# Attention and channel-mix layer: single k levels in DRAM, heads 4 to 7 held back, batch 1's features and casts moved into period 0

## The chip, the cores and the metric

One NeuronCore of a Trainium2 chip runs the whole kernel. The metric is device time in microseconds of one execution; lower is better. The engines are TensorE (PE), VectorE (DVE), ScalarE (ACT), GpSimd (POOL) and SyncE (SP, which here only issues DMAs). TensorE's clock has two levels, 2.4 GHz (granted clock 1.00) and 1.2 GHz (0.50).

## The reference, cut to what matters

The input x has 8 batches of 512 tokens by 128 channels. Attention has 16 heads of 8 channels. A score is a sum of three terms, and the softmax over it is causal:

```
q, k, v = x @ qkv_w.T                                  # (b, 16 heads, 512, 8)
scores  = alpha * tanh(q.k / beta)
scores += sigmoid(lam) * tanh(x@hex_w.T).tanh(x@hex_w.T) / 2          # "hamming", same for all heads
scores += sum_de hexc_i[d] * M_h[d,e] * hexc_j[e] / 6 * ...           # "lattice", hexc = tanh(x@q6_w.T)
x = layernorm(x + softmax(causal(scores)) @ v @ out_w.T)
r = sigmoid(mix_r(x) @ W_r.T); kk = relu(mix_k(x) @ W_k.T)**2
x = layernorm(x + r * (kk @ W_v.T))
```

## The kernel before, in words

**Levels.** To use bf16 matmuls at fp32 precision, q, k and the features are split into three bf16 levels each: hi, the cast of the whole; rest (whole minus hi); mid, the cast of the rest; lo (rest minus mid). The code has functions `hi`, `rest`, `mid`, `lo` with (batch, kind), kind being Q, K, J (features of the key side) or G (features of the query side, with the lattice map applied). VectorE does hi and mid, GpSimd rest and lo. A score matmul contracts 72 rows: 3 levels of q times 3 levels of k times 8 channels. Biases (hamming, lattice and a shift) contract 111 rows.

**The way through DRAM.** The levels lie in `parts`. SP writes them to DRAM (`to_dram`: q_rows, k_rows, j_rows, lattice_i, hamming_i) and loads them back into `q_stack`, `k_stack`, `i_stack`, `j_stack` in the order of the 72 or 111 rows (`load_stack`). Row (level l, channel d, copy c) of q_stack holds level l of q. Before, the same row of k_stack holds level (l + c) mod 3 of k, and for that k_rows has five levels (0, 1, 2, 0, 1), written in two DMAs. Heads are loaded in three groups: 0 to 3, 4 to 7, 8 to 15. A batch's stacks are double buffered.

**Steps.** A batch is 18 steps (pairs of heads), called a period. In step t TensorE runs the biases of pair t-1 on top of its scores in PSUM, the scores of pair t+1 ("ahead"), one unit of side work (`units_at`: transposes of x, projections q2, k2, features F, G, values v, and the post-attention work of the batch before) and the probability-by-value products that are due. In steps of AHEAD_FIRST the scores come ahead of the side work. Each PSUM pair has three buffers, so the scores of pair t wait until VectorE has finished pair t-3. ScalarE does tanh of pair t, then exp of pair t-3; VectorE adds scores and biases (`main`, L1210); GpSimd masks. Side units share one PSUM bank, `side_bank`: each waits until the one before has been read. The `FIRST` tables of VectorE and GpSimd say which level operation runs in which step of period 0.

**The start.** The prologue makes batch 0's levels and stacks (`first_stacks` on SP; ACT issues part of the G loads), and projects batch 1's q and k. `busy` issues matmuls whose result nobody reads. `scores(0, 0, 0)` waits for `first_qk`, the first biases for `first_g`, and `scores(0, 0, 4)` for `second_in` (heads 4 to 7 of q, k and G). The features of batch 1 are the unit F2 of the prologue, its G unit comes in step 1 of period 0. Engines run their instructions in the order written.

## Time and profile before

| | us |
|---|---|
| median of 3 runs | 377.19 |
| lowest, highest | 373.98, 377.36 |
| the profiled execution | 374.27 |
| its span, first to last instruction | 372.5 |
| mean granted clock | 0.981 |

The profiled execution is 1.77 us longer than its span and lies 2.9 us under the median of the runs; its times are in microseconds from the span's start. Period 0 is taken from its first tanh (31.03) to the first tanh of batch 1 (72.99). The timeline gives start, duration, engine, line and operation; what stands in brackets is the idle time before it and what ended it ("issue": nothing that the profile shows, which can be a DMA). A row of windows has the busy time and count of PE, PEld (weight loads), DVE, ACT and POOL, then granted clock, mean busy share of the 16 DMA engines, and GB/s.

### The profile page before, as it was taken

How to read it: one execution, taken by the hardware profiler on the slowest of the kernel's cores; microseconds unless marked ns; L12 is line 12 of the kernel's file. 1: busy time of each engine (PE TensorE's matmuls, PEld its weight loads, DVE VectorE, ACT ScalarE, POOL GpSimd, SP SyncE). 2: the span in 40 equal slices, each digit the busy share in tenths (PEclk: the TensorE clock that was granted, in tenths of full speed). 3: DMA queues.
4: the chain of work that ended last, by engine and by line, in shares of the span. 5: the costliest groups of instructions: out<-in, count | busy, mean ns of one | idle time of the engine just before them, and what ended most of it. 6: DMA issues, size and time to landing. Idle time of an engine off the chain costs nothing.

```text
span 372.5 us, 10894 instructions
## 1 busy us (share of the span) xinstructions
PE 344.4 (92%) x4181; PEld 224.4 (60%) x4181; DVE 317.2 (85%) x535; ACT 302.5 (81%) x338; POOL 241.3 (65%) x438
## 2 busy tenths in 40 slices
PE   8877896999999999999999999999999999999883
PEld 8563453566565656656576656665665666556573
DVE  4856989899999998999989999999889868976854
ACT  2322798798889978999899888997999999999712
POOL 8412848763888668865888388866885546554452
PEclk9988999899999999999999999999999999999997
DMA  4365586876763674456735775357546740210010
GB/s 114 58 219 166 178 250 192 270 220 183 198 202 102 187 203 139 128 177 194 202 117 146 182 206 163 103 161 187 157 127 185 196 136 3 59 31 2 2 30 28
DMA packets 41305, 54.01 MB, mean 145 GB/s; under 512 B 4230, under 2 KB 35974, under 8 KB 39670
## 3 DMA queue, kind: packets, MB, share of 16 engines
q1 hardware_dynamic: 36326, 50.76, 47.5%
q10 hardware_dynamic: 4928, 2.56, 2.8%
q8 instruction: 33, 0.54, 0.6%
q14 instruction: 18, 0.15, 0.1%
HBM read 38.69 MB, written 14.61 MB: 143 GB/s over the span
## 4 chain that ended last, share of the span: by engine, by line
PE 49%; DVE 15%; ACT 14%; issue 12%; POOL 8%; POOLq 0%; DVEq 0%; ACTq 0%
PE raw L556 20%; PE sums L556 12%; PE side_bank L556 12%; ACT probs L921 8%; ACT probs L916 6%; DVE probs L1210 5%; PE side_bank L684 4%; POOL probs L1090 2%; POOL x L1132 2%; POOL x L1128 2%; DVE parts L1244 2%; DVE bn L1298 1%; POOL rstd L1120 1%; DVE res L1310 1%; DVE parts L1249 1%
## 5 line engine op out<-in xcount | busy, mean ns | idle before, releaser
L1210 DVE SCALAR_TENSOR_TENSOR probs<-probs,scal,raw 128x1024 f32<-128x1024 f32 x144 | 182.1, 1274 | 19.5 <-PE raw L556 18.6
L916 ACT ACTIVATE probs<-raw 128x1024 f32<-128x1024 f32 x144 | 147.5, 1024 | 29.9 <-PE raw L556 23.8
L921 ACT ACTIVATE probs<-probs 128x1024 f32<-128x1024 f32 x144 | 151.8, 1057 | 0.0
L1090 POOL TENSOR_SCALAR_AFFINE_SELECT probs<-probs 128x128 f32<-128x128 f32 x256 | 72.6, 307 | 68.2 <-ACT probs L921 66.6
L556 PE MATMUL raw<-q_stack,k_stack 72*64 72x64 bf16 (+4 forms) x1024 | 89.2, 236 | 6.3 <-DVE probs L1210 4.7
L556 PE MATMUL raw<-i_stack,j_stack 111*128 111x64 bf16 (+4 forms) x640 | 88.4, 276 | 2.9 <-issue 1.3
L556 PEld LDWEIGHTS raw<-q_stack,k_stack 72*64 72x64 bf16 (+1 forms) x1024 | 50.1, 105 | 47.3 <-issue 21.1
L556 PE MATMUL sums<-probs,values 128*32 128x224 f32 (+3 forms) x1280 | 70.8, 343 | 1.2 <-POOL probs L1090 1.2
L556 PEld LDWEIGHTS raw<-i_stack,j_stack 111*128 111x128 bf16 (+1 forms) x640 | 46.2, 100 | 34.7 <-issue 14.1
L556 PEld LDWEIGHTS sums<-probs,values 128*32 128x32 f32 x1280 | 32.0, 109 | 29.5 <-issue 10.9
L1110 POOL TENSOR_TENSOR parts<-whole,parts 128x512 bf16<-128x512 f32 x30 | 34.8, 1167 | 6.8 <-DVE parts L1249 6.0
L1097 POOL TENSOR_TENSOR whole<-whole,parts 128x512 f32<-128x512 f32 x22 | 26.5, 1203 | 16.9 <-DVE parts L1244 16.9
L1078 POOL TENSOR_SCALAR_AFFINE_SELECT probs<-probs 128x1024 f32<-128x1024 f32 x15 | 17.2, 1149 | 5.6 <-ACT probs L921 5.6
L556 PE MATMUL sums<-ident 128*128 128x128 f32 x114 | 17.5, 313 | 1.6 <-POOL ident L1033 1.6
L1084 POOL TENSOR_SCALAR_AFFINE_SELECT probs<-probs 64x1024 f32<-64x1024 f32 x15 | 17.1, 1139 | 2.8 <-POOL probs L1078 2.8
L556 PEld LDWEIGHTS sums<-ident 128*128 128x128 f32 x114 | 16.7, 227 | 3.0 <-POOL ident L1033 1.6
L1097 POOL TENSOR_TENSOR whole<-feats,parts 128x512 f32<-128x512 f32 x8 | 9.5, 1187 | 11.9 <-DVE parts L1244 11.9
L1276 DVE COPY sums_sb<-sums 128x512 f32<-128x512 f32 x15 | 10.4, 690 | 7.9 <-PE sums L556 7.7
L1244 DVE CAST parts<-whole 128x512 bf16<-128x512 f32 x22 | 15.9, 722 | 0.2
L1120 POOL TENSOR_TENSOR rstd<-var_eps,minus_half 128x4 f32<-128x4 f32 x14 | 14.7, 1047 | 1.2
L1249 DVE CAST parts<-whole 128x512 bf16<-128x512 f32 x30 | 15.2, 524 | 0.0
L556 PE MATMUL side_bank<-w_r_mix,x1T 128*128 128x128 f32 x112 | 13.6, 275 | 0.0
(167 smaller groups left out, 399.7 us busy)
## 6 DMA issues: line engine op xcount, KB each, us to landing
q_stack<-q_rows SPq DMA_DIRECT2D x16, 288.0 KB
k_stack<-k_rows SPq DMA_DIRECT2D x16, 288.0 KB
q_stack<-q_rows SPq DMA_DIRECT2D x24, 192.0 KB
k_stack<-k_rows SPq DMA_DIRECT2D x24, 192.0 KB
i_stack<-lattice_i SPq DMA_DIRECT2D x24, 144.0 KB
i_stack<-hamming_i SPq DMA_DIRECT2D x24, 144.0 KB
i_stack<-hamming_i SPq DMA_DIRECT2D x47, 72.0 KB
i_stack<-lattice_i SPq DMA_DIRECT2D x15, 216.0 KB
```

Of the source, the lines that this page charges most:

```text
L556: return nc.tensor.matmul(o, lhsT, rhs, start=start, stop=stop, **kw)
L916: nc.scalar.activation(pair_probs(t), raw[:, t % PSUM_PAIRS, :].rearrange("p (u i) -> p u i", u=2), ACT.Tanh).then_inc(tanh_done, 1)
L921: nc.scalar.activation(pair_probs(t), pair_probs(t), ACT.Exp).then_inc(exp_done, 1)
L1078: nc.gpsimd.affine_select(out=v, in_=v, compare_op=ALU.is_ge, fill=0.0, base=SQUARE, pattern=[[0, 2 * T // SQUARE], [1, SQUARE]], channel_ ...
L1084: nc.gpsimd.affine_select(out=low, in_=low, compare_op=ALU.is_ge, fill=0.0, base=0, pattern=[[0, 2 * T // SQUARE], [1, SQUARE]], channel_m ...
L1090: last = nc.gpsimd.affine_select(out=block, in_=block, compare_op=ALU.is_ge, fill=0.0, base=SQUARE, pattern=[[0, 2], [1, SQUARE]], channel ...
L1097: nc.gpsimd.tensor_tensor(whole[:, kind, :], feats[:] if kind == J else whole[:, kind, :], parts[:, kind, 0, :], ALU.subtract).then_inc(re ...
L1110: nc.gpsimd.tensor_tensor(parts[:, kind, 2, :], whole[:, kind, :], parts[:, kind, 1, :], ALU.subtract).then_inc(lo_done[kind], 1)
L1120: nc.gpsimd.tensor_tensor(rstd[:], var_eps[:], minus_half[:], ALU.pow).then_inc(rstd_done, 1)
L1210: v.scalar_tensor_tensor(out=o, in0=o, scalar=scal[:, 2:3], in1=raw[:, t % PSUM_PAIRS, :].rearrange("p (u i) -> p u i", u=2), op0=ALU.mult ...
L1244: v.tensor_copy(parts[:, kind, 0, :], feats[:] if kind == J else whole[:, kind, :]).then_inc(hi_done[kind], 1)
L1249: v.tensor_copy(parts[:, kind, 1, :], whole[:, kind, :]).then_inc(mid_done[kind], 1)
```

## The change

- k_rows keeps three levels and is written in one DMA. A load of k_stack is now three DMAs of 24 rows each in all head groups (one of 72 rows before for heads 0 to 3 and 4 to 7): row (l, d, c) holds level l by its block, so the pairing of q and k levels is complete again, in another order.
- SP waits for all of `first_g` ahead of the loads of heads 4 to 7. The Q and K loads of heads 8 to 15 follow at once, then the write of batch 1's Q levels, then G of heads 8 to 15.
- F2 leaves the prologue; step 1 of period 0 does the features of batch 1 as F1, and G1, xT2, q2, k2 come one step later each. The two `busy(4)` around q2 and k2 go.
- In steps 1 to 3 of period 0 the scores come ahead of the side work (SCORES_AHEAD).
- VectorE's and GpSimd's FIRST tables are rearranged: batch 1's J and G casts one to two steps later, and of batch 2 hi Q at step 9 (8), hi K at 11 (10), mid K at 13, behind hi G (12, ahead of hi J).

```diff
--- before.py
+++ after.py
@@ -75,9 +75,10 @@
 AHEAD_FIRST = [3, 4, 7, 8, 9, 10, 11, 14]
 ACT_UNITS = {"k0", "G0", "F1", "F2", "kk", "rr"}
 
-FIRST_UNITS = ["xT1", "F1", "q1", "k0", "G0", "v1", "xT2", "q2", "k2", "F2"]
-
-SECOND_UNITS = {1: ["G1"], 2: ["xT2"], 3: ["q2"], 4: ["k2"], 6: ["F2"], 7: ["v1"], 13: ["G2"]}
+FIRST_UNITS = ["xT1", "F1", "q1", "k0", "G0", "v1", "xT2", "q2", "k2"]
+
+SECOND_UNITS = {1: ["F1"], 2: ["G1"], 3: ["xT2"], 4: ["q2"], 5: ["k2"], 6: ["F2"], 7: ["v1"], 13: ["G2"]}
+SCORES_AHEAD = [1, 2, 3]
 
 
 def units_at(t, post, prep, values):
@@ -128,7 +129,7 @@
 
         if n_is(n, 0) and use in ("k", "G"):
             return self.through(-1, use + "0")
-        if use == "v" or n_is(n, 0) or n_is(n, 1) and use == "G":
+        if use == "v" or n_is(n, 0) or n_is(n, 1) and use in ("F", "G"):
             return self.through(n - 1, use + "1")
         return self.through(n - 2, use + "2")
 
@@ -254,7 +255,7 @@
 
 
         q_rows = [nc.dram_tensor(f"q_rows{n}", [LEVELS, P, T], BF16, kind="Internal").ap() for n in range(2)]
-        k_rows = [nc.dram_tensor(f"k_rows{n}", [2 * LEVELS - 1, P, T], BF16, kind="Internal").ap() for n in range(2)]
+        k_rows = [nc.dram_tensor(f"k_rows{n}", [LEVELS, P, T], BF16, kind="Internal").ap() for n in range(2)]
         j_rows = [nc.dram_tensor(f"j_rows{n}", [J_ROWS, LEVELS, T], BF16, kind="Internal").ap() for n in range(2)]
         lattice_i = [nc.dram_tensor(f"lattice_i{n}", [LEVELS, NB * H, T], BF16, kind="Internal").ap()
                      for n in range(2)]
@@ -292,9 +293,9 @@
         x_in, x_second_in = sem("x_in"), sem("x_second_in")
         hi_done, mid_done = [sem(f"hi_done{n}") for n in range(4)], [sem(f"mid_done{n}") for n in range(4)]
         rest_done, lo_done = [sem(f"rest_done{n}") for n in range(4)], [sem(f"lo_done{n}") for n in range(4)]
-        SCR_DMAS = [1, 2, 1, 2]
+        SCR_DMAS = [1, 1, 1, 2]
         scr_in = [sem(f"scratch_in{n}") for n in range(4)]
-        STACK_DMAS, LAST_DMAS = [1, 1, 2, 1 + LEVELS], [LEVELS, LEVELS, 2, 2 * LEVELS]
+        STACK_DMAS, LAST_DMAS = [1, LEVELS, 2, 1 + LEVELS], [LEVELS, LEVELS, 2, 2 * LEVELS]
         stack_in = [sem(f"stack_in{n}") for n in range(4)]
 
         head_in = {kind: sem(f"head_stack_in{kind}") for kind in (Q, K, G)}
@@ -380,9 +381,7 @@
                 eng.dma_start(q_rows[par].rearrange("l p i -> p l i"), parts[:, Q]).then_inc(done, 16)
             elif kind == K:
 
-                eng.dma_start(k_rows[par][0:LEVELS].rearrange("l p i -> p l i"), parts[:, K]).then_inc(done, 16)
-                eng.dma_start(k_rows[par][LEVELS:].rearrange("l p i -> p l i"),
-                             parts[:, K, 0:LEVELS - 1]).then_inc(done, 16)
+                eng.dma_start(k_rows[par].rearrange("l p i -> p l i"), parts[:, K]).then_inc(done, 16)
             elif kind == J:
                 eng.dma_start(j_rows[par], parts[0:J_ROWS, J]).then_inc(done, 16)
             else:
@@ -393,20 +392,20 @@
         def load_stack(eng, kind, par, ready, heads=(0, H)):
 
             first, n = heads[0] * T, (heads[1] - heads[0]) * T
-            if kind in (Q, K) and heads[0] == 8:
-
-                for copy in range(LEVELS):
-                    levels = q_rows[par] if kind == Q else k_rows[par][copy:copy + LEVELS]
-                    src = levels.rearrange("l (d h) i -> (l d) (h i)", h=H)
-                    eng.dma_start((q_stack if kind == Q else k_stack)[par][copy:QK_ROWS:LEVELS, first:first + n],
-                                 src[:, first:first + n]).then_inc(ready, 16)
-            elif kind in (Q, K):
-
-                rows = q_rows[par] if kind == Q else k_rows[par]
-                level = rows[0:LEVELS].rearrange("l (d h) i -> (l d) (h i)", h=H)[:, first:first + n]
-                copies = bass.AP(level.tensor, level.offset,
-                                 [[H * T, QK_ROWS // LEVELS], [0 if kind == Q else P * T, LEVELS], [1, n]])
-                eng.dma_start((q_stack if kind == Q else k_stack)[par][:, first:first + n], copies).then_inc(ready, 16)
+            if kind == K:
+
+                for level in range(LEVELS):
+                    rows = k_rows[par].rearrange("l (d h) i -> d l (h i)", h=H)[:, :, first:first + n]
+                    at = level * LEVELS * HD
+                    eng.dma_start(k_stack[par][at:at + LEVELS * HD, first:first + n], rows).then_inc(ready, 16)
+            if kind == Q:
+                rows = q_rows[par].rearrange("l (d h) i -> (l d) (h i)", h=H)[:, first:first + n]
+                if heads[0] == 8:
+                    for copy in range(LEVELS):
+                        eng.dma_start(q_stack[par][copy:QK_ROWS:LEVELS, first:first + n], rows).then_inc(ready, 16)
+                else:
+                    eng.dma_start(q_stack[par][:, first:first + n],
+                                  rows.unsqueeze(1).broadcast_to([QK_ROWS // LEVELS, LEVELS, n])).then_inc(ready, 16)
             if kind == J:
 
                 for at, row in ((0, 0), (LAT_ROWS, HEX_J)):
@@ -507,11 +506,14 @@
                     load_stack(sp, kind, 0, first_qk, (0, 4))
                 sp.wait_ge(scr_in[G], 16 * SCR_DMAS[G])
                 load_hamming(sp, 0, first_g, (0, 4), range(LEVELS - 1))
+                sp.wait_ge(first_g, 16 * STACK_DMAS[G])
+                stand_alone(sp)
                 for kind in (Q, K, G):
                     load_stack(sp, kind, 0, second_in, (4, 8))
+                for kind in (Q, K):
+                    load_stack(sp, kind, 0, stack_in[kind], (8, H))
                 write_rows(1, 1, (Q,))
-                for kind in (Q, K, G):
-                    load_stack(sp, kind, 0, stack_in[kind], (8, H))
+                load_stack(sp, G, 0, stack_in[G], (8, H))
                 write_rows(1, 1, (K, J, G))
 
             def period(b, par, post, prep, load=True):
@@ -758,14 +760,15 @@
                     if t >= BIAS_LAG or post:
                         batch, pair = lagged(b, t, BIAS_LAG)
                         biases(batch, par if t >= BIAS_LAG else 1 - par, pair)
-                    if t in AHEAD_FIRST:
+                    first = t in AHEAD_FIRST or not post and t in SCORES_AHEAD
+                    if first:
                         ahead()
                     for use in units_at(t, post, prep, values):
                         side(b, use)
                     if post:
                         values_of(b - 1, 1 - par, t + PAIRS)
                     values_of(b, par, t)
-                    if t not in AHEAD_FIRST:
+                    if not first:
                         ahead()
 
             def transposed(out, names):
@@ -814,14 +817,11 @@
             side(-1, "v1")
             busy(12)
             side(-1, "xT2")
-            busy(4)
             side(-1, "q2")
             late_weights()
             side(-1, "k2")
-            busy(4, raw[:, 2])
             scores(0, 0, 0)
             scores(0, 0, 1)
-            side(-1, "F2")
 
             period(0, 0, False, True)
             for i in range(1, B - 4, 2):
@@ -926,8 +926,8 @@
                 if use in ("k0", "G0"):
                     ins = nc.scalar.activation(whole[:, K if use == "k0" else G, :], o, ACT.Copy)
                 elif use in ("F1", "F2"):
-                    if use == "F2":
-                        act.wait_ge(lo_done[J], b + 2)
+                    if use == "F2" or n_is(b, 0):
+                        act.wait_ge(lo_done[J], b + int(use[-1]))
                     ins = nc.scalar.activation(feats[:], o, ACT.Tanh)
                 elif use == "kk":
                     ins = nc.scalar.activation(k_act[:], o, ACT.Relu)
@@ -952,8 +952,6 @@
             def period(b, par, post, prep):
                 for t in range(PAIRS):
                     tanh(b, t)
-                    if n_is(b, 0) and t == 0:
-                        side(-1, "F2")
                     if t >= EXP_LAG or post:
                         exp(*lagged(b, t, EXP_LAG))
                     sides(b, t, post, prep)
@@ -1137,9 +1135,9 @@
                 pool.wait_ge(dve_freed, side_units.through(n + 1, "kv"))
                 nc.gpsimd.tensor_tensor(res[:], gated[:], x1[:], ALU.add).then_inc(gate_done, 1)
 
-            FIRST = {1: [(lo, 1, Q)], 2: [(rest, 1, J), (rest, 1, G)], 3: [(lo, 1, K)], 4: [(lo, 1, J)], 6: [(lo, 1, G)], 8: [(rest, 2, Q)],
-                     10: [(rest, 2, K)], 12: [(lo, 2, Q)], 13: [(lo, 2, K), (rest, 2, J)], 14: [(rest, 2, G)],
-                     16: [(lo, 2, J)], 17: [(lo, 2, G)]}
+            FIRST = {1: [(lo, 1, Q)], 2: [(rest, 1, J)], 3: [(rest, 1, G), (lo, 1, K)], 5: [(lo, 1, J)], 6: [(lo, 1, G)],
+                     9: [(rest, 2, Q)], 11: [(rest, 2, K)], 12: [(lo, 2, Q)], 13: [(lo, 2, K), (rest, 2, J)],
+                     14: [(rest, 2, G)], 16: [(lo, 2, J)], 17: [(lo, 2, G)]}
             PREP = {3: [(rest, Q)], 6: [(lo, Q)], 8: [(rest, J)], 12: [(rest, K)], 13: [(rest, G)], 14: [(lo, K), (lo, J)],
                     16: [(lo, G)]}
             POST = {9: [(inv_std, 0)], 10: [(norm, 0)], 15: [(gated_residual,)], 17: [(inv_std, 1), (norm, 1)]}
@@ -1381,9 +1379,10 @@
                 link(v.tensor_scalar(w_vT[:], sums[:, 3 * P:4 * P], 0.5, None, ALU.mult))
                 mark(DVE0_END)
 
-            FIRST = {1: [(hi, 1, J), (mid, 1, Q), (features_i, 1), (hi, 1, G)], 2: [(mid, 1, K), (x_out, 2)], 
-                     3: [(projected, 2, Q), (mid, 1, J)], 4: [(projected, 2, K)], 5: [(mid, 1, G)], 7: [(values_in, 1)], 8: [(hi, 2, Q)], 10: [(hi, 2, K)], 11: [(mid, 2, Q)], 12: [(mid, 2, K), (hi, 2, J)],
-                     13: [(features_i, 2), (hi, 2, G)], 15: [(mid, 2, J)], 16: [(mid, 2, G)]}
+            FIRST = {1: [(mid, 1, Q)], 2: [(hi, 1, J), (features_i, 1)], 3: [(x_out, 2), (hi, 1, G), (mid, 1, K)],
+                     4: [(projected, 2, Q), (mid, 1, J)], 5: [(projected, 2, K), (mid, 1, G)],
+                     7: [(values_in, 1)], 9: [(hi, 2, Q)], 11: [(hi, 2, K), (mid, 2, Q)], 12: [(hi, 2, J)],
+                     13: [(features_i, 2), (hi, 2, G), (mid, 2, K)], 15: [(mid, 2, J)], 16: [(mid, 2, G)]}
 
             parity = [0]
             v.memset(w_nat[:, 7, :], 0.0).then_inc(s_zero, 1)
```

## Rows read from the trace of the kernel before

**Rows 1.** Page: busy time; granted clock in 40 slices; tanh; VectorE's mid casts.
```profile
PE 344.4 (92%) x4181; PEld 224.4 (60%) x4181; DVE 317.2 (85%) x535; ACT 302.5 (81%) x338; POOL 241.3 (65%) x438
...
PEclk9988999899999999999999999999999999999997
...
L916 ACT ACTIVATE probs<-raw 128x1024 f32<-128x1024 f32 x144 | 147.5, 1024 | 29.9 <-PE raw L556 23.8
...
L1249 DVE CAST parts<-whole 128x512 bf16<-128x512 f32 x30 | 15.2, 524 | 0.0
```
**Rows 2.** Windows: period 0, a steady period (stretch, length, busy, clock, DMA share, GB/s).
```profile
31.03:72.99 41.96, 34.47 (x369) 18.95 (x369) 35.80 (x43) 32.81 (x36) 26.06 (x43) 0.92 0.71 213
...
193.80:234.20 40.40, 39.63 (x510) 25.49 (x507) 37.51 (x62) 36.82 (x41) 30.59 (x54) 1.00 0.61 165
```
**Rows 3.** Timeline of TensorE, end of the prologue and steps 0 to 4.
```profile
24.07 1.92 PE L556 MATMUL sums<-ident 128*128 128x128 f32 x8
...
25.78 1.85 PE L556 MATMUL side_bank<-xT,wqT 128*128 128x512 f32 x2
...
29.50 1.05 PE L556 MATMUL raw<-ident 128*128 128x128 f32 x8
...
30.39 1.04 PE L556 MATMUL raw<-q_stack,k_stack 72*128 72x64 bf16 x8
...
34.20 0.99 PE L556 MATMUL raw<-i_stack,j_stack 111*128 111x64 bf16 x4 [1.28 <-issue]
...
40.04 0.60 PE L556 MATMUL raw<-q_stack,k_stack 72*128 72x64 bf16 x4 [0.51 <-DVE probs L1210]
```
**Rows 4.** Timeline of VectorE, from the prologue to step 5.
```profile
24.32 0.69 DVE L1225 COPY xT<-side_bank 128x512 f32<-128x512 f32 x1 [0.81 <-PE side_bank L684]
...
27.73 0.75 DVE L1233 TENSOR_SCALAR whole<-side_bank,cols 128x512 f32<-128x512 f32 x1 [2.31 <-issue]
...
35.23 1.28 DVE L1210 SCALAR_TENSOR_TENSOR probs<-probs,scal,raw 128x1024 f32<-128x1024 f32 x1 [3.03 <-PE raw L556]
...
41.04 0.68 DVE L1225 COPY xT<-side_bank 128x512 f32<-128x512 f32 x1
...
45.19 0.68 DVE L1235 COPY whole<-side_bank 128x512 f32<-128x512 f32 x1
```
**Rows 5.** Timeline of the DMA queue of SP: first loads, heads 4 to 7, last heads.
```profile
24.61 0.79 SPq L409 DMA_DIRECT2D k_stack<-k_rows  x1
...
27.50 0.79 SPq L409 DMA_DIRECT2D q_stack<-q_rows  x1
...
29.96 2.33 SPq L435 DMA_DIRECT2D i_stack<-hamming_i  x3
...
41.24 2.19 SPq L401 DMA_DIRECT2D k_stack<-k_rows  x3
```
**Rows 6.** DMA issues of 19 to 21.5 us: size, us to landing.
```profile
k_rows<-parts SPq DMA_DIRECT2D x1, 384.0 KB, 3.1
...
k_rows<-parts SPq DMA_DIRECT2D x1, 256.0 KB, 4.2
```
**Rows 7.** Windows around the first biases, heads 4 to 7, and a steady period's loads.
```profile
34.00:36.00 2.00, 1.80 (x6) 1.03 (x7) 0.77 (x1) 0.47 (x1) 0.00 (x0) 0.57 0.57 166
...
37.00:38.00 1.00, 1.00 (x8) 0.66 (x7) 0.96 (x3) 0.21 (x1) 0.74 (x1) 0.66 0.02 7
...
119.00:141.00 22.00, 21.57 (x269) 13.36 (x267) 20.86 (x36) 19.38 (x22) 14.44 (x26) 1.00 0.72 201
```
**Rows 8.** Timeline of steps 12 to 15: VectorE, GpSimd and TensorE.
```profile
61.28 1.82 DVE L1249 CAST parts<-whole 128x512 bf16<-128x512 f32 x1
...
61.66 1.15 POOL L1110 TENSOR_TENSOR parts<-whole,parts 128x512 bf16<-128x512 f32 x1
...
63.45 1.26 DVE L1210 SCALAR_TENSOR_TENSOR probs<-probs,scal,raw 128x1024 f32<-128x1024 f32 x1
...
64.77 0.87 PE L556 MATMUL raw<-q_stack,k_stack 72*128 72x192 bf16 x4 [2.31 <-DVE probs L1210]
```

## The prediction

> **What bounds the kernel now.** I read the page first, then windows by period, then the timelines of single engines where the change works. TensorE is busy 92% of the span and runs at its full clock nearly everywhere; the dips sit in the first fifth [rows 1]. A steady period takes 40.4 us with TensorE busy 39.6 of them and clock 1.00: it is bound by TensorE. Period 0 is different: 41.96 us, with TensorE busy only 34.5 at a clock of 0.92, VectorE 35.8 and ScalarE 32.8 [rows 2]. It has no post-attention work and is yet the longest. So time can be won between the start of the prologue and the end of period 0 (73 us), by the waits; and because everything after it is bound by TensorE, each microsecond won or lost there reaches the end unchanged. From period 1 on the change touches DMAs alone, and there TensorE's 39.6 of 40.4 busy leaves nothing for a faster DMA to give.
>
> Four places in the first 73 us matter:
> - **The scores of pair 0** come at 30.39, behind a chain q2 (25.78), VectorE's read of it (27.73), k2, and two groups of `busy` matmuls: one ends behind the other side units (24.07 to 25.99), so that q2 starts 0.8 us after its xT is there, the other (29.50, 1.05 us) stands directly ahead of the scores [rows 3, 4].
> - **The first biases** start at 34.20 after 1.28 us in which TensorE waits for nothing that the profile shows; tanh of pair 0, which begins period 0 at 31.03, has long ended (mean of a tanh 1.02 [rows 1]), so it is `first_g`, a DMA. VectorE's first `main` at 35.23 comes after 3.03 us of waiting for them [rows 3, 4]. The loads of heads 4 to 7 are issued from 27.50 to 32.29 [rows 5] beside the G loads of heads 0 to 3 and share the DMA engines with them.
> - **The scores of pair 4** start at 40.04 when VectorE has ended `main` of pair 1, and q2 of batch 2 waits for VectorE's copy of xT at 41.04 [rows 3, 4]. From 35.23 on VectorE is the late one.
> - **Steps 12 to 15.** The cast mid K of batch 2 starts at 61.28 and takes 1.82 us, where the mean of these casts is 0.524 [rows 1, 8]; it ends 0.3 us after GpSimd's subtraction of 61.66 to 62.81. hi J and `main` of pair 12 (63.45) stand behind it, and TensorE idles 2.31 us before the scores of pair 15 at 64.77 [rows 8].
>
> **The change part by part.**
>
> *Prologue, TensorE.* Two `busy(4)` go. The copy of xT ends at 24.32 + 0.69 = 25.01 [rows 4], so q2 can start at 25.05 in place of 25.78: 0.7 us earlier. VectorE's read follows (27.0), and with it the late weights, k2 and the read of k2, all in a chain. The second `busy(4)` (1.05 us, overlapping k2's end) lets the scores follow k2. Against that stands the clock: the work removed kept TensorE busy, and k2 now probably runs partly at 1.2 GHz (q2 took 1.85 us at 25.78, most of it at that level). I take 0.7 us earlier for pair 0's scores, 0.2 to 1.2 as bounds, so 29.7. Moving F2 out costs nothing there: it stood behind the scores.
>
> *k in DRAM.* The write of two extra levels goes: 256 KB, landed at 20.44 + 4.2 = 24.6, where the first write, issued at 20.02, landed at 20.02 + 3.1 = 23.1 [rows 6]. SP waited for both, k_stack was issued at 24.61 [rows 5]. Now it can go at 23.15, but as three DMAs at 0.73 to 0.79 us each [rows 5]: issued by 25.5, against 25.40. That is a draw; `first_qk` is no later than before by more than a few tenths, and the scores at 29.7 hide it. In a steady period the K loads issue 4 DMAs more and the write 1 less: 3 x 0.76 = 2.3 us of SP. The loads of a steady period occupy 22 us (119 to 141) [rows 7] of 40, and batch b+1 needs its last heads half a period after its start; that slack of over 20 us hides it. Without it each period would pay up to 2.3 us.
>
> A rule of the Trainium skill speaks against this part ("DMA: Bandwidth & Descriptors", section on queues, rings and completion order): a DMA runs on the largest number of engines up to 16 that divides the slowest dimension of both sides. By it the new K loads run on 8 engines (channel dimension 8), the old ones on 12. The trace agrees in kind: while the loads of a steady period run, the mean DMA share is 0.72 and not 1 [rows 7]. By the rule the K part of that stretch, a quarter of 22 us, would take 1.5 times as long.
>
> *Heads 4 to 7 held back.* SP waits for `first_g`. Its last part is issued from ACT at about 27.5. Before, with the second loads beside it, it landed shortly ahead of 34.20; alone, with the small write's 3.1 us as the nearest row of an undisturbed landing and the last issues at 27.1 to 27.5, I estimate 29.5 to 30.6. The biases then wait for tanh of pair 0 instead: 29.7 + about 0.6 + 1.0 = 31.3. That is 2.9 us earlier for the first biases and 3.2 for the first `main` (32.0).
> Queued behind SP's wait are the eight DMAs of heads 4 to 7 (Q 1, K 3, G 4): 8 x 0.78 = 6.2 us of issue, so from about 29.8 to 36.0. Before, 4.8 us of issue ended at 32.29, and the flow ended between 36 and 37 us (7 GB/s in the window behind it) [rows 5, 7]. Now the end is bound by issue: 36.0 + 1.5 = 37.5, bounds 36.5 to 40.5 (a landing of 3 to 4 us as in [rows 6], and `first_g` at 30.6). Who waits: the scores of pair 4, ready since `main` of pair 1 (about 35.3), and, because step 3 puts the scores first, also xT2 behind them, VectorE's copy of it, hi G and mid K. So the wait of VectorE is replaced by a wait for `second_in`: scores of pair 4 at 37.5 against 40.04, and TensorE idle for about 1.6 us before. An idle time of 1.28 us before 34.20 was followed by a clock of 0.57 in the next 2 us [rows 3, 7], so I expect 1.2 GHz again in the next stretch. From there by hand: scores 37.5 to 38.4, xT2 to 39.6, copy to 40.3, hi G and mid K to 41.2, `main` of pair 3 to 42.4, read of q2 43.1, mid J 43.5, `main` of pair 4 44.7, read of k2 at 44.7 against 45.19 [rows 4]. So of the 3.2 us won at the first `main` only 0.5 to 1.0 is left at step 6; I take 0.7 (bounds -2.1 and +2.0).
>
> *Heads 8 to 15.* Their Q and K issue at 36.0 to 40.5, before at 38.9 to 43.4 [rows 5]; pair 9 needs them at step 8, near 50 us. G follows at 41 to 46. Both are hidden; the cover is over 4 us.
>
> *Units moved in period 0.* The same units and casts run, one step later. TensorE, VectorE and ScalarE have room there (34.5, 35.8, 32.8 of 42 us [rows 2]), and batch 1's stacks are issued at about 50, needed at 73.
>
> *Tables of steps 8 to 13.* mid K of batch 2 no longer stands between `main` of pairs 11 and 12. The excess was 1.82 - 0.52 = 1.3 us, with 0.4 of the cast itself 1.7 us. Then the scores of pair 15 start 1.6 us earlier, and the clock does not fall in front of them. Against it: GpSimd's lo K now waits for mid K at the end of step 13 and then does lo K, rest J, a mask and rest G in a row, 3 x 1.15 + 0.5 = 4.0 us, on which the masks of pairs 11 and 12 and mid J wait. I take 1.6 us, bounds -0.5 and +3.0.
>
> **Sum.** 0.7 + 1.6 = 2.3 us earlier at the end of period 0 (the 0.7 of the prologue is contained in the first term, since step 6 is reached through it). The profiled execution would be 374.3 - 2.3 = 372.0, the median 377.2 - 2.3 = **374.9 us**. The runs of before spread over 3.4 us, so a change of under 1% (3.8 us) is about what can't be told from none.
>
> **Rivals.**
> - *The held-back loads become the bound (slower).* `second_in` at 40.5 in place of 37.5. For: eight DMAs behind a wait, and small writes took 3.1 to 4.2 us to land. Against: the flow is thin by then. Everything behind the pair 4 scores is late by 3 us, less the 0.7 and 0.2 of slack: step 6 is 2.1 us later than before, and if the masks of steps 14 to 17 eat the second gain, the median is 379.3. It turns to a loss once `second_in` is later than about 38.3. Chance 0.14.
> - *Given back.* The stall of steps 12 to 15 is not removed but moved: another cast meets a GpSimd operation (three in a row are new in steps 13 and 14). Only 0.7 is left: 376.5. Chance 0.20.
> - *The early start carries through.* `second_in` lands by 36.5, the clock holds, and period 0 runs close to its VectorE work: 35.8 us less some 2 of stretched casts, plus a few unavoidable waits, 37.5 in place of 42.0. With 0.7 of the prologue about 5 us: 372.2. Chance 0.16.
> - *The narrower K loads hold the steady periods.* 2.3 us of issue more per period, of which 1 us shows in seven periods: 384. Against it the slack above. Chance 0.03. The rule of the Trainium skill named above ("DMA: Bandwidth & Descriptors", queues, rings and completion order) would add to this mechanism a slower flow of the K loads, by its figure half of a quarter of 22 us, 2.75 us, as an estimate.
> - Forecast (gain of 1 to 3.5 us): 0.47.
>
> **How the numbers follow.** Faster by over 1% needs 373.4 or less: the third rival mostly, and the upper edge of the forecast: 0.18. Slower by over 1% needs 381: the last rival and the worst of the first: 0.06. Within 1%: 0.76. The range runs from the third rival's 372 less 0.6 to the first rival's 379.3: 371.5 to 379.3.
>
> **What would show it.** Right: first `main` near 32.0; scores of pair 4 after an idle time of 1 to 2 us ended by "issue", at 37 to 38, with the clock at half behind it; k2's read in step 5 at 44 to 45; no idle time of 2 us of TensorE near 62 to 65; tanh of batch 1's pair 0 at 70.7 in place of 72.99; periods 1 to 5 at 40.2 to 40.4 as before. Wrong: `first_g` still late though nothing is beside it, pair 4 at 40 or later, or a steady period that differs at all.

## The result, and the profile after

The median is 377.83 us (17 runs, 376.18 to 379.89) against 374.27 us of the kernel before on the same chips (17 runs, 371.83 to 377.36). The ratio is 1.0102, 95% interval [1.0077, 1.0127]: the change made the kernel slower by 1%, 3.6 to 3.8 us. The median of before was 377.19 in the three runs that the prediction knew; more runs put it at 374.3, where the profiled execution was. The profiled execution of the changed kernel took 379.52 us, 1.7 us above its median, so the two profiles lie further apart (5.2 us) than the two medians (3.6 us).

The page of the changed kernel, busy times and granted clock, to be set beside [rows 1]:

```profile
span 377.7 us, 10887 instructions
...
PE 344.8 (91%) x4165; PEld 223.0 (59%) x4165; DVE 316.7 (84%) x535; ACT 302.5 (80%) x338; POOL 241.1 (64%) x438
...
PEclk9999699599999999999999999999999999999998
```

Windows of period 0 (first tanh to the first tanh of batch 1), of period 1 and of a steady period:

```profile
29.86:78.27 48.41, 38.47 (x369) 21.09 (x369) 35.07 (x43) 32.89 (x36) 27.75 (x45) 0.82 0.61 182
78.27:118.50 40.23, 39.35 (x504) 25.31 (x502) 36.83 (x55) 36.39 (x40) 26.34 (x47) 1.00 0.64 183
199.10:239.40 40.30, 39.54 (x506) 25.39 (x507) 37.43 (x61) 36.70 (x41) 30.47 (x54) 1.00 0.56 159
```

Periods 1 and later are as they were [rows 2]. Period 0 starts 1.2 us earlier and takes 48.4 us in place of 42.0, so batch 1 starts at 78.27 in place of 72.99; the 5.3 us are there at the end (span 377.7 against 372.5). TensorE's work in period 0 seems 4 us longer (38.5 against 34.5) for the same 369 matmuls: its clock was 0.82 in place of 0.92.

TensorE's timeline, where it waited and where it was slow (in brackets the idle time before and what ended it):

```profile
29.20 1.05 PE L558 MATMUL raw<-q_stack,k_stack 72*128 72x64 bf16 x8 [0.98 <-DMA k_stack<-k_rows]
31.56 0.60 PE L558 MATMUL raw<-i_stack,j_stack 111*128 111x64 bf16 x4 [1.31 <-DMA i_stack<-hamming_i]
...
40.01 1.03 PE L558 MATMUL raw<-q_stack,k_stack 72*128 72x64 bf16 x4 [4.25 <-DMA i_stack<-hamming_i]
...
62.50 1.02 PE L558 MATMUL side_bank<-feats,lat_map 128*128 128x512 f32 x2
...
65.80 0.61 PE L558 MATMUL raw<-q_stack,k_stack 72*128 72x64 bf16 x4 [2.27 <-DVE probs L1208]
...
67.60 1.03 PE L558 MATMUL raw<-q_stack,k_stack 72*128 72x192 bf16 x4 [0.75 <-DVE probs L1208]
...
74.85 2.83 PE L558 MATMUL sums<-probs,values 128*32 128x224 f32 x32
```

The first biases came at 31.56 (34.20 before). The scores of pair 0 (29.20) had waited 0.98 us for k_stack. Then the scores of pair 4 waited 4.25 us for a DMA of hamming, the last of heads 4 to 7; behind them the same four matmuls take 1.03 us in place of 0.60. There is a second stall between 63 and 68 us (2.27 and 0.75 us idle), and the 32 value matmuls of step 17 take 2.83 us at 74.85, where before they took 1.61 at 70.79.

SP's DMA queue tells why (compare [rows 5]):

```profile
23.32 2.07 SPq L400 DMA_DIRECT2D k_stack<-k_rows  x3
25.43 1.62 SPq L434 DMA_DIRECT2D i_stack<-hamming_i  x2
31.56 0.79 SPq L407 DMA_DIRECT2D q_stack<-q_rows  x1
32.40 2.08 SPq L400 DMA_DIRECT2D k_stack<-k_rows  x3
34.52 0.77 SPq L427 DMA_DIRECT2D i_stack<-lattice_i  x1
35.33 2.33 SPq L434 DMA_DIRECT2D i_stack<-hamming_i  x3
```

SP stood from 27.05 to 31.56 for `first_g`; the eight DMAs took until 37.66 (35.33 + 2.33) to issue, and 2.35 us more to land. VectorE's and GpSimd's timelines (compare [rows 4, 8]):

```profile
32.20 1.28 DVE L1208 SCALAR_TENSOR_TENSOR probs<-probs,scal,raw 128x1024 f32<-128x1024 f32 x1 [1.44 <-PE raw L558]
...
41.94 0.69 DVE L1223 COPY xT<-side_bank 128x512 f32<-128x512 f32 x1 [4.60 <-PE side_bank L686]
...
47.56 0.69 DVE L1233 COPY whole<-side_bank 128x512 f32<-128x512 f32 x1
...
62.01 1.14 POOL L1082 TENSOR_SCALAR_AFFINE_SELECT probs<-probs 64x1024 f32<-64x1024 f32 x1 [0.17 <-POOL probs L1076]
62.04 2.51 DVE L1247 CAST parts<-whole 128x512 bf16<-128x512 f32 x1
...
63.12 1.15 POOL L1095 TENSOR_TENSOR whole<-whole,parts 128x512 f32<-128x512 f32 x1
```

`main` of pair 0 is 3.0 us earlier than before, the read of k2 (47.56) 2.4 us later. And mid Q of batch 2, now in step 11, takes 2.51 us: it starts with one GpSimd operation and ends 0.3 us after a second one that follows without a gap (63.12 + 1.15 = 64.27).

### The profile page after: what moved, and what is told of

Same layout as the page of the kernel before. It is cut to its first block, busy times and chain, and to the rows that moved or that the text cites. A ratio compares the mean times of both kernels' runs of the same rounds, so it can differ in the third digit from the quotient of the medians.

```text
span 377.7 us, 10887 instructions
## 1 busy us (share of the span) xinstructions
PE 344.8 (91%) x4165; PEld 223.0 (59%) x4165; DVE 316.7 (84%) x535; ACT 302.5 (80%) x338; POOL 241.1 (64%) x438
## 4 chain that ended last, share of the span: by engine, by line
PE 48%; ACT 14%; DVE 11%; issue 10%; POOL 9%; DMA 4%; SPq 3%; POOLq 0%; DVEq 0%; ACTq 0%
PE raw L558 21%; PE side_bank L558 12%; PE sums L558 10%; ACT probs L921 8%; ACT probs L916 6%; DVE probs L1208 4%; PE side_bank L686 4%; DMA i_stack<-hamming_i 2%; POOL probs L1088 2%; POOL x L1130 2%; POOL x L1126 2%; DVE parts L1242 2%; DMA probs<-in_L_attn_hex_w 1%; SPq L400 1%; DVE bn L1296 1%
## 5 line engine op out<-in xcount | busy, mean ns | idle before, releaser
L916 ACT ACTIVATE probs<-raw 128x1024 f32<-128x1024 f32 x144 | 147.2, 1024 | 34.3 <-PE raw L558 29.5
L558 PE MATMUL raw<-q_stack,k_stack 72*64 72x64 bf16 (+4 forms) x1024 | 90.5, 239 | 11.3 <-DVE probs L1208 4.5
L558 PE MATMUL raw<-i_stack,j_stack 111*128 111x64 bf16 (+4 forms) x640 | 89.7, 279 | 3.0 <-DMA i_stack<-hamming_i 1.3
L558 PE MATMUL sums<-probs,values 128*32 128x224 f32 (+3 forms) x1280 | 72.1, 348 | 1.2 <-POOL probs L1088 1.2
L1095 POOL TENSOR_TENSOR whole<-feats,parts 128x512 f32<-128x512 f32 x8 | 9.3, 1165 | 12.5 <-DVE parts L1242 12.5
L558 PE MATMUL sums<-ident 128*128 128x128 f32 x106 | 15.1, 298 | 1.6 <-POOL ident L1031 1.6
L558 PEld LDWEIGHTS sums<-ident 128*128 128x128 f32 x106 | 14.4, 213 | 3.0 <-POOL ident L1031 1.6
L1118 POOL TENSOR_TENSOR rstd<-var_eps,minus_half 128x4 f32<-128x4 f32 x14 | 14.6, 1046 | 1.2
L1242 DVE CAST parts<-whole 128x512 bf16<-128x512 f32 x22 | 15.2, 691 | 0.1
L1247 DVE CAST parts<-whole 128x512 bf16<-128x512 f32 x30 | 15.0, 515 | 0.0
```

The source lines that it names most:

```text
L558: return nc.tensor.matmul(o, lhsT, rhs, start=start, stop=stop, **kw)
L916: nc.scalar.activation(pair_probs(t), raw[:, t % PSUM_PAIRS, :].rearrange("p (u i) -> p u i", u=2), ACT.Tanh).then_inc(tanh_done, 1)
L1095: nc.gpsimd.tensor_tensor(whole[:, kind, :], feats[:] if kind == J else whole[:, kind, :], parts[:, kind, 0, :], ALU.subtract).then_inc(re ...
L1242: v.tensor_copy(parts[:, kind, 0, :], feats[:] if kind == J else whole[:, kind, :]).then_inc(hi_done[kind], 1)
L1247: v.tensor_copy(parts[:, kind, 1, :], whole[:, kind, :]).then_inc(mid_done[kind], 1)
```

## The experiments

Each was timed beside the kernel before on its own chip. The interval of a ratio is 0.2 to 0.4% to either side (0.8% for old_k, with four runs), so two ratios can be told apart only when they differ by some 0.4 to 0.6%. K is the single k levels, H the wait that holds heads 4 to 7 back, S the moved steps (with tables and removed `busy`). no_hold, old_k, old_steps and everything called "the change" also have the new order of heads 8 to 15, which was not tried by itself.

| run | what it is | ratio to before, 95% |
|---|---|---|
| k_only | K | 0.9956 [0.993, 0.9983] |
| k_only_again | K | 0.9973 [0.995, 0.9996] |
| hold_only | H | 1.0016 [0.9983, 1.0049] |
| steps_only | S | 1.0048 [1.0026, 1.0071] |
| old_steps | K, H | 1.0004 [0.9968, 1.004] |
| no_hold | K, S | 1.0022 [0.9982, 1.0063] |
| old_k | H, S | 1.012 [1.0042, 1.0197] |
| the change | K, H, S | 1.0102 [1.0077, 1.0127] |
| xt_first | the change, repeated | 1.0084 [1.0049, 1.0119] |
| split_wait | the change, Q and K of heads 4 to 7 awaited apart from G | 0.9969 [0.9931, 1.0007] |
| keep_warm | the change, busy(16) ahead of the wait | 1.0047 [1.0008, 1.0086] |
| xt_ahead | the change, xT2 ahead of pair 4 in step 3 | 1.0032 [1.0001, 1.0063] |
| old_tables | the change, old entries of steps 8 to 13 | 1.0079 [1.0047, 1.0112] |
| casts_early | the change, hi K and mid Q of batch 2 in step 10 | 1.0029 [0.9996, 1.0061] |
| split_early | split_wait and casts_early | 0.9968 [0.9939, 0.9998] |
| split_tables | split_wait and old_tables | 0.9984 [0.9954, 1.0014] |
| xt_ahead_split | split_wait and xt_ahead | 0.9994 [0.9964, 1.0023] |
| k_split | K and split_wait, nothing else | 0.9953 [0.9914, 0.9993] |

**One part away at a time.** H out of the changed kernel:

```diff
                 load_hamming(sp, 0, first_g, (0, 4), range(LEVELS - 1))
-                sp.wait_ge(first_g, 16 * STACK_DMAS[G])
-                stand_alone(sp)
```

> The changed kernel without SP's wait for first_g. Theory A (the held-back loads are the loss): heads 4 to 7 are issued from about 27 us, the scores of pair 4 start near 37 in place of 40.0, TensorE's idle time before them falls from 4.25 us to under 2, and the end comes 3 to 5 us earlier: ratio to the kernel before 0.995 to 1.003. Rival B (the moved steps and tables are the loss): the first biases slip back to about 34, the stall near 62 stays, ratio still 1.008 to 1.012.

The ratio was 1.0022, and in the profile the wait of pair 4 fell from 4.25 to 2.43 us (scores at 39.43), not to under 2 as I expected; the first biases came at 32.79 without any hold-back, 1.2 us later than with it. So the wait costs about 0.8% here (with both intervals, 0.3 to 1.3%), and gives only 1.2 of the 2.6 us by which the biases are early.

K out:

```diff
-        k_rows = [nc.dram_tensor(f"k_rows{n}", [LEVELS, P, T], ...
+        k_rows = [nc.dram_tensor(f"k_rows{n}", [2 * LEVELS - 1, P, T], ...
-        SCR_DMAS = [1, 1, 1, 2]
+        SCR_DMAS = [1, 2, 1, 2]
-        STACK_DMAS, LAST_DMAS = [1, LEVELS, 2, 1 + LEVELS], [LEVELS, LEVELS, 2, 2 * LEVELS]
+        STACK_DMAS, LAST_DMAS = [1, 1, 2, 1 + LEVELS], [LEVELS, LEVELS, 2, 2 * LEVELS]
```

> The changed kernel with the five-level k_rows and one K DMA per head group of 4. Theory A2 (three K DMAs behind the wait make it worse): eight issues become six, second_in lands 1.3 us earlier, pair 4 starts near 38.7 and the ratio falls by 0.3% to about 1.006. Rival: the wait for first_g moves later by as much, because the second k write (256 KB) is back ahead of it, and the ratio stays at 1.010.

The ratio was 1.012, where the rival had it, though its interval (1.0042 to 1.0197) takes in the 1.006 of the theory too; the profile decides. The eight issues became six, but `first_g` landed at 32.76 in place of 31.56, and although the last issue ended at 37.57, as in the change (37.66), pair 4 started only at 42.58, after 5.61 us of waiting. So putting one K DMA in place of the three narrow ones did not bring the held-back loads in earlier. Why they landed 5.0 us behind the last issue and not 2.35 is open. S out (steps, tables and `busy` as in the kernel before):

> The changed kernel with the steps, tables and busy matmuls as before: single k levels, held-back loads and the new order of heads 8 to 15. If the parts add (0.9956 for k, +0.008 for the wait), ratio 1.002 to 1.006. Rival: with the features in the prologue VectorE has work during the wait for pair 4, and the wait costs less: 0.996 to 1.000.

The ratio was 1.0004. Against K alone (0.9956 and 0.9973, below) the wait, with the new order of heads 8 to 15, costs 0.3 to 0.5% when S is out, and 0.8% when it is in; the intervals overlap, so this difference by itself is not shown. The parts alone, each put into the kernel before as the diff has it:

> The kernel before with SP's wait for first_g alone. Theory A says that this wait costs what the change lost: pair 4 waits for heads 4 to 7 until about 40 to 42, ratio 1.006 to 1.015. Rival: it costs only beside the three K DMAs or the moved steps, ratio 0.998 to 1.004. Then the first biases come at 31 to 32 in either case.

The ratio was 1.0016, the rival's; the first biases came at 32.63, 1.6 us early, and pair 4 waited 3.26 us there too and started at 40.66.

> The kernel before with the moved steps, tables, scores ahead and removed busy matmuls alone; k_rows, the loads and their order as before. From the runs so far: single k levels alone 0.9956, changed kernel without the wait 1.0022, so the steps should cost 0.004 to 0.008: ratio 1.004 to 1.008, with the longer stall (2.27 and 0.75 us idle) near 62. Rival (the steps are neutral and it is the two earlier landings that clash): 0.998 to 1.002.

1.0048 was measured, as expected: S costs by itself. Pair 4 came at 38.65 with no wait at all.

> The kernel before with the single k levels alone (three K DMAs, one write less). Theory (the k part is neutral): ratio 0.998 to 1.002, steady periods 40.3 us. Rival (narrower K loads hold something in each period): 1.005 or more, with the loss spread over the periods. Where no hold-back stands in front, first_qk lands about 1.5 us earlier and second_in up to 1 us later than before.

> The kernel before with the single k levels alone, a second time with more rounds, as the candidate for a version faster than both: ratio 0.994 to 0.998 if 0.9956 was no accident; 0.999 to 1.001 if it was.

K gains: 0.9956 and 0.9973. TensorE's timeline of k_only shows where:

```profile
31.81 0.60 PE L554 MATMUL raw<-i_stack,j_stack 111*128 111x64 bf16 x4
...
37.54 0.61 PE L554 MATMUL raw<-q_stack,k_stack 72*128 72x64 bf16 x4 [0.95 <-DMA i_stack<-hamming_i]
```

The first biases start at 31.81 with nothing held back, directly behind the side unit before them, 2.4 us earlier than before [rows 3], and pair 4 at 37.54.

**The wait itself.** Into the changed kernel (split_wait): Q and K get a semaphore of their own, and the biases of pair 4 wait for G:

```diff
-                    load_stack(sp, kind, 0, second_in, (4, 8))
+                    load_stack(sp, kind, 0, second_in if kind == G else second_qk, (4, 8))
 ...
-                    pe.wait_ge(second_in, 16 * (STACK_DMAS[Q] + STACK_DMAS[K] + STACK_DMAS[G]))
+                    pe.wait_ge(second_qk, 16 * (STACK_DMAS[Q] + STACK_DMAS[K]))
```

> The changed kernel, where the scores of pair 4 wait for Q and K of heads 4 to 7 alone and the biases of pair 4 for G. Theory A: Q and K are issued by 34.5 and land by 36.5 to 37, so pair 4 starts about 3 us earlier, TensorE's idle time is 1 us, ratio 0.997 to 1.003. Rival: G of heads 4 to 7 (landing at 39.7) now stops the biases of pair 4 one step later, and only 1 us is gained: 1.007.

```profile
37.78 0.61 PE L560 MATMUL raw<-q_stack,k_stack 72*128 72x64 bf16 x4 [1.41 <-DMA k_stack<-k_rows]
```

Pair 4 is 2.2 us earlier than 40.01, and at the full clock; the ratio was 0.9969, so the whole loss is gone. The biases of pair 4 did not wait for G. The clock by itself (keep_warm):

```diff
                 elif first and t == 4:
+                    pe.wait_ge(s_dve0, DVE0_END)
+                    busy(16)
                     pe.wait_ge(second_in, ...)
```

> The changed kernel with busy(16), about 3.7 us of matmuls that nobody reads, in front of the wait for heads 4 to 7. Pair 4 still starts at 40.0. If the half clock from 40 to 47 us is a cost of its own, the read of k2 comes at about 45.3 to 46.0 in place of 47.56 and the ratio falls to 1.004 to 1.006. Rival: VectorE is the late one behind pair 4 anyway, and the ratio stays at 1.009 to 1.010.

```profile
35.29 3.74 PE L558 MATMUL sums<-ident 128*128 128x128 f32 x32
40.43 0.61 PE L558 MATMUL raw<-q_stack,k_stack 72*128 72x64 bf16 x4 [1.40 <-DMA i_stack<-hamming_i]
```

The same wait with useless matmuls in it: pair 4 is no earlier, but its matmuls take 0.61 us and not 1.03. k2's matmul comes 1.4 us earlier (44.78 in place of 46.16) and its read at 46.41, later than the 45.3 to 46.0 expected; the ratio fell to 1.0047, only just clear of 1.0102. What stands behind the wait (xt_ahead):

```diff
-                    first = t in AHEAD_FIRST or not post and t in SCORES_AHEAD
+                    first = t in AHEAD_FIRST if post or t > 3 else t in (1, 2)
```

A first attempt set SCORES_AHEAD to [1, 2] and changed nothing, because step 3 is in AHEAD_FIRST as well; it counts as a repeat of the changed kernel.

> The changed kernel with SCORES_AHEAD = [1, 2]: in step 3 xT2 goes ahead of the scores of pair 4, so it and VectorE's copy, hi G and mid K run during the wait for heads 4 to 7. Theory D (the hold-back costs 0.8% beside the moved steps and 0.2% without them because the moved steps put this work behind the wait): the read of k2 comes 1.0 to 1.5 us earlier than 47.56 and the ratio is 1.005 to 1.008. Rival (only the length of the wait counts): 1.009 to 1.011.

> The changed kernel with xT2 really ahead of the scores of pair 4 in step 3 (the run before this one left the order as it was, since step 3 is in AHEAD_FIRST). Theory D: xT2, VectorE's copy, hi G and mid K then run during the wait for heads 4 to 7; the read of k2 comes 1.0 to 1.5 us earlier than 47.56, ratio 1.004 to 1.008. Rival (only the length of the wait and the clock count): the copy is early, the end is not, 1.008 to 1.011.

The ratio was 1.0032, which speaks for theory D. VectorE's timeline of xt_ahead:

```profile
39.56 0.68 DVE L1223 COPY xT<-side_bank 128x512 f32<-128x512 f32 x1
...
44.73 0.68 DVE L1233 COPY whole<-side_bank 128x512 f32<-128x512 f32 x1
```

The copy of xT is done at 40.2 and the read of k2 at 44.73, 2.8 us earlier than 47.56, although pair 4 itself started at 40.15. TensorE idled 0.99 us there and not 4.25, since xT2 came in between and its matmuls from 31 to 37 us happened to be at the lower clock (0.51). Behind pair 4 the clock was 1.00, so this profile does not separate the order of the units from the clock.

**The second stall.** The edit of casts_early, in VectorE's table; old_tables puts the entries of steps 8 to 13 back in both tables:

```diff
-  9: [(hi, 2, Q)], 11: [(hi, 2, K), (mid, 2, Q)], 12: [(hi, 2, J)],
+  9: [(hi, 2, Q)], 10: [(hi, 2, K), (mid, 2, Q)], 12: [(hi, 2, J)],
```

> The changed kernel with the FIRST entries of steps 8 to 13 of VectorE and GpSimd as before. In all four runs so far with the new entries the cast mid Q of batch 2 (step 11) takes 2.51 us, and TensorE idles 2.27 and 0.75 us behind it; with the old ones, before, the two casts took 0.89 and 1.82 and TensorE idled 2.31 once. Theory C (the new entries lengthen this stall, and the clock falls for 10 us behind it): 1 to 3 us less, ratio 1.002 to 1.007. Rival: the stall is as long with either table, only placed otherwise, ratio 1.009 to 1.011.

> The changed kernel with hi K and mid Q of batch 2 in step 10 of VectorE in place of 11, where GpSimd is idle (58.9 to 60.7 us in the changed kernel). Theory C (a VectorE cast that starts while GpSimd works ends only when GpSimd pauses): both casts take 0.42 us, the stall near 62 us is gone, no half clock near 67, 3 to 5 us less: ratio 0.998 to 1.003. Rival (TensorE's idle time there comes of the order of the units, not of the cast): the cast is short and the idle time stays, ratio 1.008.

The old tables gave 1.0079, which can't be told from 1.0102. The casts in step 10 gave 1.0029. Its VectorE timeline:

```profile
60.03 0.42 DVE L1242 CAST parts<-whole 128x512 bf16<-128x512 f32 x1
60.36 0.42 DVE L1247 CAST parts<-whole 128x512 bf16<-128x512 f32 x1
...
66.04 1.10 DVE L1242 CAST parts<-whole 128x512 bf16<-128x512 f32 x1
```

In GpSimd's pause the casts take 0.42 us each; later ones (66.04) are stretched in turn. The stall is not gone, though the expectation had it gone: TensorE still idles 2.39 us (0.36, 1.29 and 0.74) from 65 to 71 us, in place of 3.02, but its clock stays at 1.00. Windows behind the stall, of the changed kernel and of casts_early:

```profile
70.00:74.00 4.00, 4.00 (x57) 2.54 (x50) 3.53 (x5) 3.38 (x4) 3.60 (x7) 0.50 0.58 181
74.00:78.00 4.00, 4.00 (x40) 1.76 (x39) 2.13 (x3) 1.97 (x3) 3.52 (x6) 0.58 0.60 182
```

```profile
70.00:74.00 4.00, 3.40 (x76) 2.06 (x78) 4.00 (x4) 3.35 (x5) 4.00 (x9) 1.00 0.83 276
```

In 4 us there are 57 matmuls at clock 0.50 (1.2 GHz) and 76 at 1.00 (2.4 GHz), of partly different steps. This does not yet show that the change brings the half clock. xt_first, the changed kernel a second time, has the same stall and the full clock behind it:

```profile
62.79 1.02 PE L558 MATMUL side_bank<-feats,lat_map 128*128 128x512 f32 x2
...
66.09 0.61 PE L558 MATMUL raw<-q_stack,k_stack 72*128 72x64 bf16 x4 [2.27 <-DVE probs L1208]
...
67.89 0.61 PE L558 MATMUL raw<-q_stack,k_stack 72*128 72x192 bf16 x4 [0.75 <-DVE probs L1208]
...
73.43 1.61 PE L558 MATMUL sums<-probs,values 128*32 128x224 f32 x32
```

Before the change:

```profile
60.30 1.02 PE L556 MATMUL side_bank<-feats,lat_map 128*128 128x512 f32 x2
...
70.79 1.61 PE L556 MATMUL sums<-probs,values 128*32 128x224 f32 x32
```

Take the stretch from the start of G's matmuls of step 13 (feats and lat_map) to the end of the value matmuls of step 17. It begins at 60.30 before and at 62.50 in the changed kernel, so 2.2 us are lost ahead of it. It lasts 12.1 us before and 15.2 in the changed kernel, 3.1 us more, but in xt_first only 12.3. So with the clock up all the way the moved entries still cost this stretch 0.2 us against before (where the clock was 0.70 from 66 to 70 us), and the other 2.9 are a half clock that one execution of a program shows and another does not: K alone has 11.9 us in k_only and 14.6 in k_only_again. Of the nine profiles with the new entries (casts_early and split_early apart) five have a long stretch (14.8 to 15.2 us) and four a short one (12.3 to 12.5); of the eight with the old entries one is long (14.6), the others have 11.7 to 12.1. That the new entries bring the long one more often is suggested, not shown. casts_early has 10.2 us. In steps_only the stretch begins at 60.24, as before, and lasts 14.9: the whole 2.7 us by which its span is longer stand there.

**Combinations.**

> Both repairs: the split wait for heads 4 to 7 and the casts in step 10. If the two losses are separate and add, ratio 0.997 - 0.007 = 0.988 to 0.993, faster than both kernels. If one hides the other (TensorE bound from step 7 on), 0.995 to 0.997.

> The changed kernel with the split wait and the old FIRST entries of steps 8 to 13. If the new entries cost 0.2% (1.0102 against 1.0079) beside the wait's 1.3% (1.0102 against 0.9969), ratio 0.993 to 0.996. Rival: the new entries cost only where the clock stays down for 10 us behind their stall, which it does not in the split wait's run (3.4 us), and the ratio is 0.996 to 0.998.

> The same with the split wait. If the two repairs add, ratio 0.993 to 0.996; if VectorE or TensorE is the late one from step 4 on anyway, 0.996 to 0.998 as with the split wait alone.

> The kernel before with the single k levels and the split wait for heads 4 to 7; no hold-back, steps as before. In the run with the k levels alone pair 4 waited 0.95 us for G of heads 4 to 7, with a half clock behind it. Without that wait 0.5 to 1.5 us less: ratio 0.992 to 0.995, the fastest version. Rival: VectorE is the late one again at pair 4 and nothing is gained beyond 0.9956.

The repairs don't add: with the split wait in, neither the casts, the old tables nor xT2 ahead brings anything that can be measured (0.9968, 0.9984, 0.9994 against 0.9969). So H and S bring nothing that can be measured even where their wait is mended: split_wait, with K, H and S, has 0.9969, K alone 0.9956 and 0.9973. The lowest ratios are those of the single k levels alone, twice below 1, and with the split wait (0.9953), which can't be told from them: 373.2 to 373.7 us against 374.7, faster than both kernels by 0.3 to 0.5% and 1.3 to 1.5%.

## Why the prediction was wrong

The forecast was 2.3 us faster, the measured change is 3.6 us slower (377.83 against 374.27). That 377.83 lies in the range of 371.5 to 379.3 is luck: the range was counted from 377.2, the median of three runs, where seventeen runs gave 374.27. Counted from there its upper end, 2.1 us slower, is 376.4. What happened is the first rival, and beside it what the second one names: the stall of steps 12 to 15 was moved and not removed.

- **What bounds the kernel: right.** Steady periods did not change, and the loss of period 0 reached the end (5.3 us at the start of batch 1, 5.2 at the end).
- **Prologue, 0.7 us earlier: right.** It was 1.2 in these two profiles (29.20), but this start differs by over 1 us between profiles; the six with the old prologue have a median of 30.2 us, the thirteen with the new one 29.4. k2 even kept its full clock in this profile. That `first_qk` would be hidden was wrong: the scores waited 0.98 us for k_stack.
- **k in DRAM, "a draw": wrong, it was the part that gained.** I compared the issue times of k_stack (25.5 and 25.40) and stopped there. The second write of 256 KB stood also ahead of the other first loads; with single levels the biases come at 31.81 (32.39 in k_only_again) with no further change. Whether the missing write does this or the new form of the loads, no run separates. I credited the same 2.9 us to the hold-back, which in fact brought 1.2 beside K and S (31.56 with it, 32.79 without) and 1.6 alone.
- **Heads 4 to 7 held back: the step that failed**, with the term `second_in` at 37.5. It was to be 29.8 for `first_g`, 6.2 of issue and 1.5 of landing. Measured: 31.56, 6.10 and 2.35, so 40.01. I had reckoned the landing of `first_g` from a single undisturbed write, though it is four DMAs behind those of q_stack and k_stack. That this is why it was late is my reading, no run tests it. The upper bound of 40.5 held. With that the rival's own arithmetic came out: read of k2 at 47.3 by its 2.1 us, 47.56 measured. That this wait is a cause of the loss, split_wait shows: with Q and K awaited by themselves the ratio is 0.9969 in place of 1.0102.
- **What is behind the wait: half seen.** I named xT2, its copy, hi G and mid K, and the clock. Both are part of the price: with xT2 ahead of the blocked scores the ratio falls from 1.0102 to 1.0032, with the clock kept up to 1.0047, though pair 4 comes no earlier in either. Before the change xT2 stood in step 2, ahead of pair 4. The wait costs 0.8% with S and 0.2 to 0.5% without, which agrees but is within the intervals. I should have asked whether moving the units and adding the wait work against each other.
- **Tables of steps 8 to 13, 1.6 us: wrong in sign.** mid K no longer stood between `main` of pairs 11 and 12, as forecast, but mid Q of step 11 met two GpSimd operations in a row (2.51 us). "Another cast meets a GpSimd operation" was the rival Given back, at no loss; TensorE idled 2.27 + 0.75 us in place of 2.31. The stretch of steps 13 to 17 became 0.2 us longer with the clock up (xt_first), in place of 1.6 us shorter.
- **The clock behind the second stall was left out.** It was 0.50 from 70 to 74 us and 0.58 from 74 to 78, where before it was 1.00 there (0.70 from 66 to 70). It makes 2.9 us of this profile's loss, but xt_first had 1.00 from 66 to 78 us, so it is no fixed part of the change.
- **The narrow K loads in the steady periods: rightly given 0.03.** k_only is faster as a whole, and from 70 to 180 us its TensorE is busy 107.9 of 110 us at clock 1.00. The rule of the Trainium skill on the number of engines ("DMA: Bandwidth & Descriptors", in the section on why a DMA increments its semaphore by 16, and not in the one that I named) thus changed no time that can be measured here. Whether the new K loads ran on 8 engines no view shows; if they did, the slack covers it.

What stays open: how much of the 1% is the second stall. Alone, casts_early says 0.7% (with both intervals, 0.3 to 1.1%), old_tables 0.2% (none within the intervals), and beside the split wait neither says anything. The stretch at half clock behind that stall differs between profiles of nearly the same program: in the two runs of the single k levels, which are one program, the clock of 66 to 70 us was 0.84 in one and 0.50 in the other.

## What to carry to other kernels

A wait added on a DMA queue costs what is queued behind it plus what its consumer's engine has in order behind the consumer: look for the side work that could run ahead of the blocked instruction (here xT2 and its copy), and wait for each operand at its own first use (here 1.3% of the time). Reckon a landing from all the DMAs that must land, not from the shortest row. Where TensorE's clock falls behind a stall, as here behind both, the stall can be paid a second time; one profile of each kernel does not say whether the change or the execution brought it, so look at a second profile of the same program. Count a forecast from more than three runs when they spread by more than the change is to bring.

## What the runs showed of the hardware

- A VectorE cast from fp32 to bf16 of 128x512 takes 0.42 us when GpSimd is idle. If it starts while GpSimd works on a tile of 512 or 1024 columns it ends about 0.3 us after that operation (0.89 us before, 59.28 to 60.17 behind an operation that ended at 59.89), or, if GpSimd starts another such operation without a gap, 0.3 us after that one (2.51 us). So did all of the about 300 such casts in the nineteen profiles. The short masks of 128x128 hold it little: hi J at 63.02 before took 0.51 us beside two of them; but mid K at 61.28 before began beside masks, met the subtraction that followed them without a gap, and took 1.82 us. A cast that started first, with GpSimd's operation 0.2 us behind, took its 0.42 us (108 casts). `main` took 1.25 to 1.28 us in the profiles of both kernels, beside GpSimd or not. Which resource they share, no view shows.
- Granted clock and time go together loosely from run to run. Of the changed kernel's 17 runs the fastest had clock 0.987 and 376.18 us, and seven had 0.968 and 377.37 to 379.72; but 0.983 gave 377.35 and 0.973 gave 379.52 and 379.70.
- How long the clock stays down after a like stall differs between executions of one program. Behind idle times of 2.27 and 0.75 us it was 1.00 from 66 to 78 us in xt_first, while in the changed kernel it was 0.50 from 70 to 74 us with TensorE busy all of that time.
